# A fused attention and expert layer: all early weight splits in one row, gates by a power on GpSimd, ring slots in another order

## The reference, cut to what matters

```python
# attention, per head: weights sin/cos of the place in the sequence
q = relu(x @ Wq.T + bq); k = relu(x @ Wk.T + bk); v = x @ Wv.T + bv
q_ = concat([q * sin, q * cos]); k_ = concat([k * sin, k * cos])
kv = einsum('nld,nlm->ndm', k_, v)
z = 1.0 / maximum(einsum('nld,nd->nl', q_, k_.sum(axis=1)), EPS)
x = layernorm(x + (einsum('nld,ndm->nlm', q_, kv) * z) @ Wo.T + bo)
# experts
logits = x @ router_w.T
topv, topi = top_k(logits, 2);  w = softmax(topv)
for e in range(8):
    out += gate[:, e:e+1] * (gelu(x @ w1[e].T) @ w2[e].T)
x = layernorm(x + out)
```

## Time and profile before

| | |
|---|---|
| median of 3 runs | 949.94 us |
| profiled execution | 946.41 us, span 944.6 us |
| PE busy | 873.7 us, 92% |
| DVE, ACT, POOL busy | 595.3, 507.2, 411.3 us |
| chain that ended last | PE 75%, DVE 13%, ACT 3%, POOL 3%, issue 3%, DMA 2% |
| largest lines of the chain | 684 (19%), 671 (17%), 485 (8%) |
| first phase | until about 350 us |
| steps with groups between | about 353 to 640 us |

### The profile page before, as it was taken

One profiled execution on the slowest core, in us unless ns is written; L12 is line 12 of the kernel. 1 busy time (PEld: TensorE's weight loads), 2 busy tenths in 40 slices (PEclk: granted clock), 3 DMA queues, 4 the chain that ended last, 5 costly groups with the idle time before them and its releaser, 6 DMA issues.

```text
span 944.6 us, 20681 instructions
## 1 busy us (share of the span) xinstructions
PE 873.7 (92%) x5845; PEld 773.1 (82%) x5845; DVE 595.3 (63%) x1896; ACT 507.2 (54%) x1045; POOL 411.3 (44%) x527
## 2 busy tenths in 40 slices
PE   6999998999899978899999999999999999999980
PEld 5888987898788967788888898888888888887870
DVE  4336778777877785566666666664444444577774
ACT  4566665666566654455555556553343343446665
POOL 4641445644576483443544454452222222234443
PEclk9999999999999999999999999999999999999995
DMA  5351223322232233222323332232322222567764
GB/s 179 122 157 34 92 90 113 102 95 93 101 98 78 81 129 91 85 81 67 97 92 91 97 90 78 69 105 72 118 74 74 69 79 68 207 203 250 250 247 191
DMA packets 55952, 106.42 MB, mean 113 GB/s; under 512 B 9133, under 2 KB 37423, under 8 KB 53808
## 3 DMA queue, kind: packets, MB, share of 16 engines
q1 hardware_dynamic: 40736, 62.84, 21.8%
q0 software_dynamic: 12672, 33.84, 9.9%
q10 hardware_dynamic: 2448, 8.52, 2.4%
HBM read 61.76 MB, written 44.45 MB: 112 GB/s over the span
## 4 chain that ended last, share of the span: by engine, by line
PE 75%; DVE 13%; ACT 3%; POOL 3%; issue 3%; DMA 2%; SPq 0%; ACTq 0%; DVEq 0%; POOLq 0%
PE PS L684 19%; PE PS L671 17%; PE PS L485 8%; PE PS L696 5%; PE PS L499 5%; PE PS L570 5%; PE PS L552 4%; PE PS L514 4%; PE PS L660 3%; PE PS L531 2%; DVE den L1014 1%; DVE o L1018 1%; PE PS L523 1%; POOL token_rows L1559 1%; POOL zrs L1567 1%
## 5 line engine op out<-in xcount | busy, mean ns | idle before, releaser
L1559 POOL DMA_INDIRECT token_rows<-y,xg x136 | 136.3, 1002 | 334.7 <-DVE y L1327 306.4
L684 PEld LDWEIGHTS PS<-w,hT 128*128 128x128 f32 x1632 | 210.4, 191 | 34.2 <-issue 29.4
L684 PE MATMUL PS<-w,hT 128*128 x1632 | 229.9, 290 | 1.8 <-DVE hT L1377 1.5
L671 PE MATMUL PS<-w,xgT 128*128 x816 | 222.6, 408 | 0.0
L1483 POOL DMA_INDIRECT expert_rows<-rows,idx x128 | 126.3, 987 | 104.6 <-DVE idx L1125 66.7
L671 PEld LDWEIGHTS PS<-w,xgT 128*128 128x128 f32 x816 | 143.5, 189 | 24.6
L944 ACT ACTIVATE hT<-PS 128x512 fp32r<-128x512 f32 x136 | 81.4, 598 | 141.8 <-PE PS L696 141.8
L940 ACT ACTIVATE hg<-PS 128x512 f32<-128x512 f32 x136 | 81.3, 597 | 134.5 <-PE PS L671 132.7
L1377 DVE TENSOR_TENSOR hT<-PS,hT 128x512 fp32r<-128x512 f32 x136 | 94.0, 691 | 65.3 <-ACT hT L944 64.9
L1318 DVE TENSOR_TENSOR xgT<-PS,xgT 128x256 fp32r<-128x256 f32 x136 | 57.5, 423 | 119.8 <-ACT xgT L911 119.5
L485 PE MATMUL PS<-wkv,xs 128*128 128x512 f32 x384 | 109.2, 421 | 9.2 <-DVE wkv L1274 9.2
(11 more groups left out here) (165 smaller groups left out, 1376.4 us busy)
## 6 DMA issues: line engine op xcount, KB each, us to landing
xg<-expert_rows SPq DMA_DIRECT2D x136, 130.0 KB, 2.1
z<-token_rows SPq DMA_DIRECT2D x16, 1024.0 KB, 6.6
xraw<-in_xT SPq DMA_DIRECT2D x32, 256.0 KB
xtok<-in_x SPq DMA_DIRECT2D x32, 256.0 KB, 2.7
out_y<-z ACTq DMA_DIRECT2D x16, 512.0 KB, 3.0
wraw<-in_w1T SPq DMA_DIRECT2D x7, 512.0 KB, 3.9
wraw<-in_w2T SPq DMA_DIRECT2D x7, 512.0 KB, 3.7
token_rows<-y,xg POOLq DMA_INDIRECT x136, 2.5
```

Of the source, the lines that this page charges most:

```text
L671: mm = nc.tensor.matmul(PS[:, gH, :], xgT[:, s % 2, a, k, :], w[:, bass.ds(e, 1), b, k * F:(k + 1) * F].rearrange("p o f -> p (o f)"), sta ...
L684: mm = nc.tensor.matmul(PS[:, gY, 0:D], hT[:, a, k, :], w[:, bass.ds(e, 1), b, HALF + k * D:HALF + (k + 1) * D] .rearrange("p o f -> p (o ...
L1559: nc.gpsimd.indirect_dma_start(yd, bass.IndirectOffsetOnAxis(ap=xg[:, (s + XG_FIRST) % NXG, C_DST:C_GATE].bitcast(U32), axis=0), y[:, s % ...
```

## The change

- POOL splits halves 0 to 12 one after the other ahead of its first repetition, and half 13 in repetition 10. Its own pipeline begins at repetition 8, since there is nothing else for it before. SP's loads are placed by a table (`HALVES_LOADED_AT`), up to two in a repetition, and its first batch is written out instead of looped.
- The low part of the last w1 half goes from POOL to DVE, as one instruction (`late_low`).
- In the steps el is e^2 to the power dl, computed on POOL with `pow` from a new constant; ACT computes no Exp there. In the first phase it still does. ACT runs one Gelu on two elements at the phase's end.
- The ring slots are used in the order 2, 3, 4, 0, 1, 5, 6, 7 instead of 2, 3, 4, 5, 6, 7, 0, 1. The gather of step 3 waits for the last states' matmuls, and only that of step 5 for state_split.
- The scatters of pair 22 stand after the sends of steps 5 and 6 instead of all four after that of step 4.

```diff
-        def pipeline(eng, step):
+        def pipeline(eng, step, begin=0, unrolled=4):
...
-            for i in range(4):
+            for i in range(begin, unrolled):
                 once(i)
-            loop(4, PB - 1)
+            if unrolled < PB:
+                loop(unrolled, PB - 1)
...
-        XG_FIRST = 2
+        XG_SLOTS = (2, 3, 4, 0, 1, 5, 6, 7)
...
+        HALVES = 2 * EARLY
+        LAST_HALF_AT = LAG + 1
+        HALVES_LOADED_AT = {2: (2,), 3: (3, 4), 4: (5,), 5: (6,), 6: (7, 8), 7: (9,), 8: (10, 11), 9: (12,), 10: (13,)}
...
-                before = weight_expert_before(u, rep)
-                if before is not None and rep - 1 < 3 * PB + 2:
-                    sp.wait_ge(wprep, before * 4 + (2 * (1 - par) + 2))
-                    sp.dma_start(wraw[:, 1 - par], w_experts[1 - par][before + 1]).then_inc(s_wraw[1 - par], 16)
-
-            pipeline(sp, step)
+                for n in HALVES_LOADED_AT.get(rep, ()) if rep < PB + 4 else ():
+                    sp.wait_ge(wprep, 2 * (n - 1))
+                    sp.dma_start(wraw[:, n % 2], w_experts[n % 2][n // 2]).then_inc(s_wraw[n % 2], 16)
+
+            pipeline(sp, step, unrolled=PB)
...
                 if s == 3:
+                    sp.wait_ge(st_done, 2 * NPAIR)
+                if s == 5:
                     sp.wait_ge(state_step, STATE * B)
...
-            pe.wait_ge(wprep, 4 * EARLY + 3)
+            pe.wait_ge(wprep, 4 * EARLY + 2)
+            pe.wait_ge(late_low, 1)
...
+            nc.scalar.activation(gelu_first[:], half_neg[:, 0:2], ACT.Gelu, scale=2.0)
             act.wait_ge(s_late[0], 16)
             act.wait_ge(kv_done, 2 * NPAIR)
...
             rows_high(0)
-            gate_power(A - 2)
...
                     if n == 2:
                         attention_high(j, rep)
-                        gate_power(j - 1)
...
             choose(A - 2, G - 2)
+            dve.wait_ge(late_high, 1)
+            nc.vector.tensor_tensor(w[:, EARLY, 1, 0:HALF], w_late_raw[:, 0, 1, 0:HALF], w[:, EARLY, 0, 0:HALF].bitcast(F32),
+                                    ALU.subtract).then_inc(late_low, 1)
             residual(A - 1, 0, biased=A - FIRST_TOKEN_BIAS)
...
+            nc.gpsimd.memset(e_square[:], math.exp(2.0)).then_inc(pool_const, 1)
...
+            def weight_half(n):
+
+                e, kind = n // 2, n % 2
+                pool.wait_ge(s_wraw[kind], e * 16 + 16)
+                c0 = kind * HALF
+                w_hi, w_lo = (w[:, e, part, c0:c0 + HALF] for part in range(2))
+                nc.gpsimd.tensor_copy(w_hi, wraw[:, kind]).then_inc(wprep, 1)
+                pool.wait_ge(wprep, 2 * n + 1)
+                for c in range(0, HALF, D):
+                    a = nc.gpsimd.tensor_tensor(w_lo[:, c:c + D], wraw[:, kind, c:c + D], w_hi[:, c:c + D].bitcast(F32),
+                                                ALU.subtract)
                 a.then_inc(wprep, 1)
...
+                if rep == LAST_HALF_AT:
+                    weight_half(HALVES - 1)
...
-            pipeline(pool, step)
+            pool.wait_ge(proj_low, 4)
+            for n in range(HALVES - 1):
+                weight_half(n)
+            pipeline(pool, step, begin=PB, unrolled=PB)
...
-            late_weight(0)
+
+            def gate_power(jj):
+                pool.wait_ge(route_step, jj * ROUTE + ROUTE_DL)
+                nc.gpsimd.tensor_tensor(el[:], e_square[:], dl[:], ALU.pow).then_inc(e_ready, 1)
+
             token_bias(A, A // 2, 1)
+            gate_power(A - 2)
             half_deviation(A - 1)
...
+                j, n = hook(s)
+                if s == 3:
+                    gate_power(A - 1)
+                if n == 1:
+                    gate_power(NPAIR - 1 if j is None else j - 1)
                 send(s)
                 if s == 4:
                     half_deviation(A)
-                if s == 4:
-                    scattered(A - 1)
-                    for n in range(4):
-                        scatter(0, n // TOPK, n % TOPK)
-                j, n = hook(s)
+                if 5 <= s <= 6:
+                    if s == 5:
+                        scattered(A - 1)
+                    for k in range(TOPK):
+                        scatter(0, s - 5, k)
```

More of the change, by code:

```diff
@@ L17 @@
+import math
 from contextlib import ExitStack
@@ L120, in build @@
         half_neg = sb("half_neg", [4])
+        e_square = sb("e_square", [2])
+        gelu_first = sb("gelu_first", [2])
         ones_bf = sb("ones_bf", [P], BF16)
@@ L259, in build @@
         xghi_ready, gelu_ready, hhi_ready = sem("xghi_ready"), sem("gelu_ready"), sem("hhi_ready")
-        qhi_ready = sem("qhi_ready")
+        qhi_ready, late_low = sem("qhi_ready"), sem("late_low")
         dve_const, proj_low, ones_ready, o_done = sem("dve_const"), sem("proj_low"), sem("ones_ready"), sem("o_done")
@@ L272, in build @@
         wprep, pow_step, zpow_step = sem("wprep"), sem("pow_step"), sem("zpow_step")
-        POOL_CONST = 10
+        POOL_CONST = 11
         BIAS, BIAS_OUT = 4, 7
@@ L414, in gather @@
                 row = nc.values_load(steps[1:2, place:place + 1], engines=[ENG.SP], min_val=0, max_val=E * REGION)
[L415 removed]
+                sp.dma_start(xg[:, XG_SLOTS[s % NXG]], ex[bass.ds(row, P), :]).then_inc(s_xg[s % NXG], 16)
             def freed(s):
@@ L660, in rows_transposed @@
                     mm = nc.tensor.transpose(PS[:, gX, k * P:(k + 1) * P],
-                                             xg[:, (s + XG_FIRST) % NXG, k * P:(k + 1) * P], ident)
+                                             xg[:, XG_SLOTS[s % NXG], k * P:(k + 1) * P], ident)
                 mm.then_inc(tx_done, 1)
@@ L1489, in token_bias, with late_weight @@
                     .then_inc(xb_ready, 1)
-            def late_weight(kind):
-                raw = w_late_raw[:, 0, 1, kind * HALF:(kind + 1) * HALF]
-                high = w[:, EARLY, 0, kind * HALF:(kind + 1) * HALF]
-                if kind == 1:
-                    pool.wait_ge(s_late[1], 16)
-                    pool.wait_ge(kv_done, 2 * NPAIR)
-                    nc.gpsimd.tensor_copy(high, raw).then_inc(wprep, 1)
-                    pool.wait_ge(wprep, 4 * EARLY + 1)
-                else:
-                    pool.wait_ge(late_high, 1)
-                low = w[:, EARLY, 1, kind * HALF:(kind + 1) * HALF]
+            def late_weight():
+                raw = w_late_raw[:, 0, 1, HALF:]
+                high, low = w[:, EARLY, 0, HALF:], w[:, EARLY, 1, HALF:]
+                pool.wait_ge(s_late[1], 16)
+                pool.wait_ge(kv_done, 2 * NPAIR)
+                nc.gpsimd.tensor_copy(high, raw).then_inc(wprep, 1)
+                pool.wait_ge(wprep, 4 * EARLY + 1)
                 for c in range(0, HALF, D):
                     a = nc.gpsimd.tensor_tensor(low[:, c:c + D], raw[:, c:c + D], high[:, c:c + D].bitcast(F32), ALU.subtract)
+                a.then_inc(wprep, 1)
+            def weight_half(n):
[8 more added lines that the diff above has]
+                                                ALU.subtract)
                 a.then_inc(wprep, 1)
@@ L1525, in step @@
                     half_deviation(j - 1)
-                e = weight_expert(u, rep)
-                if e is not None:
-                    pool.wait_ge(s_wraw[par], e * 16 + 16)
-                    if rep == 2:
-                        pool.wait_ge(proj_low, 4)
-                    c0 = par * HALF
-                    w_hi, w_lo = (w[:, bass.ds(e, 1), part, c0:c0 + HALF].rearrange("p o f -> p (o f)")
-                                  for part in range(2))
-                    nc.gpsimd.tensor_copy(w_hi, wraw[:, par]).then_inc(wprep, 1)
-                    pool.wait_ge(wprep, e * 4 + (2 * par + 1))
-                    for c in range(0, HALF, D):
-                        a = nc.gpsimd.tensor_tensor(w_lo[:, c:c + D], wraw[:, par, c:c + D], w_hi[:, c:c + D].bitcast(F32),
-                                                    ALU.subtract)
-                    a.then_inc(wprep, 1)
+                if rep == LAST_HALF_AT:
+                    weight_half(HALVES - 1)
                 if rep == NPAIR - 1:
-                    late_weight(1)
+                    late_weight()
                 if route:
```

15 lines of the change are left out of this document (2 added, 13 removed).

## The result

The changed kernel takes 935.5 us (median of 4 runs, 934.25 to 937.75), the kernel before in the same set 949.5 us (4 runs, 948.16 to 950.97). The ratio is 0.9856, with a 95% interval of 0.9832 to 0.9881: 14.0 us faster. The profiled execution took 934.87 us (a span of 933.0) where that of before took 946.41, so the two traces explain 11.5 us. The other 2.5 us lie between profiled executions and medians: the median is 3.1 us above the profiled execution before and 0.6 us after. Here and in the experiments the ratios leave out the few slow executions (such as one of 976.09 us, at a granted clock of 0.84, of the version with a pause in repetition 8), while the medians have them in.

A forecast was written before the change was run, and what follows sets the result against it. TensorE bounds the kernel, so only its waits or lower clock count. Weights 5.1, change of phase 4.2 and gates 2.6 give about 12.0 us: profiled 934.4, median 937.9 us, own range 933 to 942, 8 in 10 range 930 to 945.

The forecast's parts named there:

- Repetition 8: POOL's early splits stretch DVE's chain before the first attend: six instructions at 0.4 us, less slack, PE waits 1.8 us.
- The second rival: Early splits cost more: repetition 8 waits 4.8 us instead of 1.8 and the clock falls; 942 to 943.5 us, chance 0.18.
- the two give back 4.4 us: Repetitions 16 and 24: without POOL's split beside it, DVE's chain is 2.2 us shorter in each.
- net 5.1 us for the weights: First phase: 7.7 us from late splits that leave, less 1.8 in repetition 8 and 0.8 in repetition 10.
- Change of phase: Between first phase and steps: step 0 starts 0.6 us earlier, step 2 gains 3.0 including it, clock 1.2; together 4.2 us.
- then PE reads the expert's number, 1.2 us: Before step 0, PE still spends 1.2 us on this read after its last attend, so only 0.6 us is gained.
- The 1.2 us of clock: Step 2: with a wait of about 1 us instead of 3.3, PE keeps full clock, 1.2 us more.
- Gates: Step 3 and the second step after the last group lose PE waits of 1.16 and 1.43 us: 2.6 us gained.
- PE has outputs of the step before meanwhile: In the steps, DVE waits about 0.6 us longer for the power, but PE's outputs work hides it.
- The first rival: PE's wait in the eight groups goes too, worth 9.3 us: 928.6 us, chance 0.12.
- third: Slower: POOL reaches the power late and DVE waits in every group, 20 us in ten places: 958 us, chance 0.04.
- fourth rival: Late loads leave POOL waiting, splits run into repetitions 9 to 11, the 5.1 us are lost: 943 us, chance 0.06.

The follow-up runs named there:

- the version with a pause in repetition 8: Changed kernel with 11 instead of 13 weight halves split ahead of POOL's repetitions, halves 11 to 13 in repetitions 9 to 11: 935.12 us, ratio 0.9824.
- the second set: Runs of the changed kernel with token_bias ahead of its send, half_deviation ahead of step 4's send, splits paused, or all three; the kernel before took 949.9 us there.
- the gates alone: Kernel before with only el as a power on POOL instead of Exp, one first Gelu, and pair 22's scatters in steps 5 and 6: 1003.04 us, ratio 0.9866.
- the slots alone: Kernel before with only the new ring slot order and the changed wait of step 3's gather; w1's last low part stays on POOL: ratio 0.9993.
- the change of phase alone: Kernel before with only w1's last low part on DVE, the new ring slot order and the changed wait of step 3's gather: ratio 0.994.

## Why the prediction was right, and where not

**The sum** held: 937.9 was forecast, 935.5 came, within the forecast's own range. By the trace 11.5 us of the 12.0 are there; that the median is 2.4 us below the forecast comes from its distance to the profiled execution, which was carried over as 3.5 us and came out as 0.6. The terms are less good than the sum, and that it came out so close is in part luck: 2.1 us lost on steps 5 to 9 and 1.4 on repetitions 16 and 17 beyond the forecast stand against 0.8 at the start, 0.9 in steps 1 to 4, and 1.7 in the groups that nobody forecast.

**Repetitions 0 to 8.** Nothing for 0 to 7 was right (6.15 us for each, as before). The 0.8 us at the start are not the change's: repetition 8 begins at 60.56 us here, at 61.37 before, and at 61.4 to 63.2 in the four traces of the second set, whose code is the same up to there. Repetition 8 (1.8 forecast, 2.0 in the trace) was right in its size and its cause: the pause took it away. How it is made up was not right: four instructions were stretched by 0.56 us on average, not six by 0.4 (which would be 2.4 and not 2.3), and POOL did rest, 0.73 us for a load. The second rival, that it costs more and the clock falls behind it, did happen in two of six traces (6.7 and 6.9 us instead of 5.2), so its chance of 0.18 was low for that part of it, though the other parts hold.

**Repetitions 16 and 17** gave 1.6 us, not 3.0. The step that failed is "the two give back 4.4 us", which carried the difference of two DVE chains over to PE. PE's wait for pos did shrink by 2.2 us in both places, and the slow clock behind it went too, so that 16 by itself gave 3.7 us and 24 gave 3.4 (from first bias matmul to first bias matmul). But the next wait, for aT behind state_split, had been hidden: it was none in 17 and 0.24 us in 25 and is now 1.59 us in both (160.93), in 17 with a slow clock behind it (0.70 in 160 to 165 us). So 17 took back 2.4 us and 25 took back 0.5; the 1.4 us that "stay" in 24 stay in 25. The distances that the prediction named as signs, 11.7 us in 17 and 25 and 13 in 16 and 24, came out as 14.8, 13.2 and 12.0, 12.0; in 26 and 27 it was 11.6. 24 to 27 gave 5.1 for 4.7, but 3.5 to 3.6 in three further traces and 1.9 in a fourth, all with the same instructions there, since the clock fell once more. Of the net 5.1 us for the weights the profiled execution of the changed kernel shows 4.1, and that with token_bias moved 2.3: 2.2 and 0.6 lost in 8 and 10, 1.5 and 3.6 gained.

**Change of phase.** Step 0 came 1.0 us earlier, not 0.6. The step that failed is "then PE reads the expert's number, 1.2 us". In all five traces with POOL's low part as before, PE starts step 0 1.21 to 1.23 us behind its end; with late_low done early, PE waits 0.23 us there. So what takes the 1.2 us (by the program's order the reading) is hidden behind the attend unless PE's queue waits for something first. For step 2 the next in line was named rightly (xgT of DVE, a wait of 1.0 us), and step 2 began 3.3 us earlier for 3.0. The 1.2 us of clock were there, but by a wrong reason: the run with the gates alone kept the 3.4 us wait and full clock.

**Gates.** Step 3 gave 1.4 us for 1.16 (5.7 us from its hg to the next with the slots alone or the change of phase alone, 4.3 with the gates alone). Step 56 gave 0.8 for 1.43: the new wait for the power (610.33, 0.44 us) is not hidden there, since rows_low stands behind it in the same step, and PE waits 0.88 us. "PE has outputs of the step before meanwhile" failed at that place. Steps 5 to 9 lost 2.1 us: the wait for half_deviation stayed, as predicted, but the clock fell behind it, 1.5 of the 2.1 us. Taking the wait away gave 4.4 us.

**Groups.** Nothing was forecast, 1.7 us came, 0.2 for each: with ACT free, the hg after position 2 comes 0.75 us earlier and the next step gives 0.5 of it back. By the prediction's own sign ("if the groups got shorter") it was wrong there. The first rival (the wait goes too) did not come, for the reason that was given: token_bias stayed behind send. The run with token_bias ahead of the send shows that it was this, in seven groups. "The wait is alike in the groups" was not so in the third, where the clamp was free even before.

The third and fourth rival left next to no trace: DVE waits for the power 0.44 us in two places; POOL waits for four loads, 1.6 us in all, and its thirteenth half ended at 69.7 us for 71 forecast. There is one table load for Gelu in all, as forecast.

## What to carry to other kernels

When two engines share SBUF, ask of every instruction on the idle engine which instruction of the other it will lie beside: moving a 1.3 us addition of POOL by 1.8 us was worth 1.1 us in seven of eight groups, where the removal of 16 table loads went with 0.2 us in each. When a wait is taken away, look for the one hidden behind it before its whole length is counted. A long row of work on an engine that seems idle wants a pause where its neighbour has its one tight chain (2.0 us here, 1.1 net in the trace). And what a slow clock behind a wait costs is not a term of a sum but a chance: the same wait had it in one trace and not in the next.

## What the runs showed of the hardware

**SBUF contention.** DVE's clamp of 32 columns took 0.18 us alone and 1.43 us when it began within 0.1 us of POOL's addition of 512 columns (1.32 us), so it ended with it. It was held although its start stands first in the trace, by 0.05 us in the rows of the second group above. In the third group with token_bias ahead of the send it began 0.65 us ahead of the addition, beside a scatter, and took 2.00 us, again until the addition was done (446.90 to 448.90 us, the addition 447.55 to 448.84). In the changed kernel the clamp of the third group began beside a scatter and took 0.18 us. Why it was held in the one case and not in the other was not found. Low parts of 512 columns went from 0.69 to 1.21 us beside POOL's subtractions, and four of POOL's own from 2.81 to 3.80 us. The Trainium skill, GPSIMD Engine Reference (Specifications), says that the SBUF interfaces are shared by GpSimd and VectorE, with contention for VectorE instructions with two SBUF inputs; the low parts have two, and the trace agrees.

**The clock behind a wait.** The changed kernel and the one with half_deviation moved have the same instructions until step 4. In repetition 8 one waits 1.46 us and goes on at full clock, the other 1.93 us and has a mean of 0.66 over the next 5 us, so it ran in part at the lower level of 1.2 GHz (the changed kernel first):

```profile
70.00:75.00 5.00, 4.96 (x31) 4.22 (x29) 2.35 (x7) 3.22 (x8) 0.00 (x0) 1.00 0.16 52
```

```profile
70.00:75.00 5.00, 5.00 (x19) 4.37 (x20) 1.80 (x4) 2.74 (x7) 1.20 (x2) 0.66 0.03 13
```

Length alone is not what decides. In repetition 8 the full clock stayed over the next 5 us behind waits of 1.46, 1.57, 1.70 and 1.98 us in four traces and not behind 1.79 and 1.93 us in two. Behind the wait of 2.4 us before step 6 it stayed in three traces, the kernel before among them, and was 0.66 to 0.71 in eight, the changed kernel among them. In step 2, 3.41 us left it full with the gates alone, while 3.34 us had not. What decides was not found.

**A table load** took 1.28 us, and the next activation began 0.02 us after its end; ahead of the 21 loads in the steps of the kernel before ACT was idle for 0.4 us in all. So no further cost of the switch is to be seen:

```profile
341.10 1.28 ACT L904 ACT_TABLE_LOAD   x1
...
342.40 0.20 ACT L904 ACTIVATE gelu_first<-half_neg 128x2 f32<-128x2 f32 x1
```

**Open.** Why two sets took 6.6 to 6.8% longer, with idle times of ACT and DVE that have no releaser, why the gates gain more beside them, and why the version with token_bias one position earlier is nearly free of them in the groups, was not settled.
